# Shared low-rank factors laid out twice and rounded in three steps for four, and two unread matmuls behind the first factor mix

## Chip, cores, metric

One core of one Trainium2 chip. The metric is the device time of the whole kernel in microseconds (us), as a median over runs. PE is the matmul engine, PEld its weight loads, DVE, ACT and POOL the vector, scalar and GpSimd engines, and SP the engine whose queue issues nearly all DMA transfers.

## Reference

```
h = grouped_conv1d(x, weight) + (cond @ c_weight.T)[:, :, None] + fside[None, :, None]   # 64 rows n, 64 channels, 1024 long
A_eff = einsum('bn,nri->bri', gate, lora_A);  B_eff = einsum('bn,nor->bor', gate, lora_B)  # 8 b, rank 32
out = x + h @ kernel + bias + B_eff(A_eff h) + B_shared(A_shared h)                      # 1024 x 1024 kernel
```

The shared factors don't depend on the row, so the kernel adds B_shared · A_shared to the dense weights once (this is what `merge` does).

## The kernel before

The 64 rows are worked in 8 blocks `b` of 8 rows; each has two halves `h` of two groups `t`. Products in float32 are made from a high part (rounded to the matmul's fp32r format) and a low part (the rest): ACT rounds to the high part, DVE or POOL subtracts to get the low part, and PE makes three products, high·high, high·low and low·high. Nothing is scheduled by a program: each engine has its own queue, written out by hand, with waits on semaphores, and every engine works its queue in order.

A first stage, some 60 us long, prepares the weights while the first block is worked. Names that matter here:

- `load_la(q)`, `load_first(half)`, `load_w(ma)` on SP: loads of the per-adapter A factors (four quarters `la`), of the first block's input (`x_tr`) and of the dense weights (`w_raw`). The order on SP is small inputs, `la` 0, first half of the input, shared factors `sh_in`, `la` 1 to 3, weights 0 and 1, second half of the input, bias, weights 2 and 3, B factors.
- `mix_a(q)` (L879) on PE: quarter `q` of the gated sum of A factors into `main` (in PSUM); `a_turn(q)` on DVE turns it into `a_eff`. Quarter 0 goes to `main[1][:, 0:512]`, quarter 1 to `main[1][:, 512:1024]`.
- `x_first_high` on ACT rounds the first input into `x_hi` (two instructions of 128x528, `t` 0 and 1); `x_lo` is made for `t` 0 by DVE and for `t` 1 by POOL. `convolve` (L819) is then 12 matmuls for one tile of the convolution.
- `as_st` and `bs_st` are the two operands of `merge`. `as_st` holds rows A high, A low, A high (32 partitions each), `bs_st` B high, B high, B low, so that one matmul over 96 partitions sums the three products. `sh_in` has A in its partitions 0 to 31 and B in 32 to 63. ACT makes the four high parts in four instructions of 32 partitions (`shared_high`, L445), then POOL makes A low (`as_lo`, L339) and B low (`bs_lo`, L343).
- `merge(m)` (L867) needs all of these; DVE's `w_add(m)` adds its result to `w_raw`, ACT's `w_high(k)` and POOL's `w_low(k)` split it, and `chunk(k)` on PE uses it: 12 matmuls of 512 columns.

On PE the order at the start is: two unread matmuls on `ident`, the conditioning product, the tap transposes, `mix_a(0)`, two `convolve`, `mix_a(1)`, `mix_a(2)`, `merge(0)`, `merge(1)`, `mix_a(3)`, `merge(2)`, `merge(3)`, `chunk(0)`, and so on.

Of the kernel before, what the change touches and what calls it, by code (L numbers as in the profile page):

```python
# [8 lines left out]
ACT = mybir.ActivationFunctionType  # L9
AX = mybir.AxisListType  # L10

P = 128
# [4 lines left out]
NL, R = 16, 32  # L17
# [8 lines left out]
STACK = 3 * R  # L26
# [25 lines left out]
def adaln_ffn(nc, x, x_rows, x_first, small, conv_w, kern, bias, lora_a, lora_b, shared, out):  # L52
# [9 lines left out]
    with ctx:  # L62
# [3 lines left out]
        def ps(name, shape):  # L66
            return ctx.enter_context(nc.psum_tensor(name, shape, F32))

        def sem(name):
            return ctx.enter_context(nc.semaphore(name))  # L70

        def early(*specs):

            with ExitStack() as own:
                return [own.enter_context(nc.sbuf_tensor(*s)) for s in specs]
# [5 lines left out]
        z_all, as_st, bs_st = early(("z_all", [C, WIN, CG, J], F32), ("as_st", [P, KC, P], F32R), ("bs_st", [P, D], F32R))  # L81
        y_hi1, y_lo1 = sb("y_hi1", [P, 2, KC, P], F32R), sb("y_lo1", [P, 2, KC, P], F32R)
        sh_in, bias_nat, bias_hi, bias_lo = early(("sh_in", [P, D], F32), ("bias_nat", [16, 64], F32),
                                                 ("bias_hi", [16, 64], F32R), ("bias_lo", [16, 64], F32R))
        _, t01_raw = early(("res_front3", [P, 2, D], F32), ("t01_raw", [P, G, J, CG], F32))
        _, be_raw = early(("res_front", [P, 2, D], F32), ("be_raw", [P, RQ, 512], F32))
        _, be_lo = early(("res_front2", [P, 2, D], F32), ("be_lo", [P, RQ, 512], F32R))
        res = sb("res", [P, G, D])
        la, = early(("la", [P, RQ, L], F32))
# [19 lines left out]
        ident, gmix = early(("ident", [P, P], F32), ("gmix", [P, NB, R8], F32))  # L109
# [3 lines left out]
        main = [ps(f"main{i}", [P, D]) for i in range(2)]  # L113
# [5 lines left out]
        cw_in, small_in, shared_in = sem("cw_in"), sem("small_in"), sem("shared_in")  # L119
# [7 lines left out]
        diag_done, gmix_done, bs_hi, bs_lo = sem("diag_done"), sem("gmix_done"), sem("bs_hi"), sem("bs_lo")  # L127
        as_hi, as_lo = sem("as_hi"), sem("as_lo")
# [60 lines left out]
        def w_bank(m):  # L189
            return (spare, rank)[m % 2][:, :]  # L190
# [4 lines left out]
        def a_out(q):  # L195
            return main[1 - q // 2][:, (q % 2) * 512:(q % 2 + 1) * 512].rearrange("p (b k m) -> p b k m", b=2, m=32)
# [3 lines left out]
        def load_first(eng, half):  # L200
            m0, m1 = ((0, XSPLIT), (XSPLIT, MB))[half]
            eng.dma_start(x_tr[:, m0:m1, :, :].rearrange("p m n g -> p (m n g)"),
                          x_first[0, :, m0 * SB * G:m1 * SB * G]).then_inc(x_first_in[half], 16)
# [8 lines left out]
        def _(sp):  # L212
            sp.dma_start(sm[:, :], small).then_inc(small_in, 16)
            load_la(sp, 0)
            load_first(sp, 0)
            sp.dma_start(sh_in[0:2 * R, :], shared).then_inc(shared_in, 16)
            for q in range(1, RQ):
                load_la(sp, q)
            load_w(sp, 0)
# [28 lines left out]

            sp.wait_ge(as_lo, 1)
            sp.wait_ge(bs_lo, 1)  # L250
            sp.wait_ge(as_hi, 2)
            sp.wait_ge(bs_hi, 2)
            load_res(0, 0)
            sp.wait_ge(bias_put, 32)
# [12 lines left out]
            for i, (part, split) in enumerate(((be_hi, be_hid), (be_lo, be_lod))):  # L267
                sp.wait_ge(split, RQ)
                for oh in range(2):
                    for bq in range(2):  # L270
                        row = oh * 64 + bq * R
# [170 lines left out]
        def _(act):  # L442
            act.dma_start(w_nat[:, :], conv_w.rearrange("o c k -> o (c k)")).then_inc(cw_in, 16)

            def shared_high(q):  # L445

                row, at = ((0, R), (2 * R, 0))[q]
                nc.scalar.activation(as_st[row:row + R, :, :].rearrange("p k m -> p (k m)"), sh_in[0:R, :], ACT.Copy).then_inc(as_hi, 1)
                nc.scalar.activation(bs_st[at:at + R, :], sh_in[R:2 * R, :], ACT.Copy).then_inc(bs_hi, 1)

            for w in range(2):
                act.wait_ge(t_tr, w + 1)
                nc.scalar.activation(t_hi[:, :, w * J:(w + 1) * J, :].rearrange("p g s c -> p s g c"),
# [11 lines left out]
                                 main[0][:, 512:1024].rearrange("p (s g c) -> p s g c", s=J, g=G), ACT.Copy).then_inc(t01_copied, 1)  # L465
            x_first_high(0)
            act.wait_ge(shared_in, 16)
            shared_high(0)
            shared_high(1)

            def y_high_first(u, i, order):
                t, mh = order[i]
# [325 lines left out]
        def _(pe):  # L798
            mm = nc.tensor.matmul
# [19 lines left out]
            def convolve(b, h, i, order=ORDER, first=False):  # L819
                u = b * 2 + h  # L820
                t, mh = order[i]
                if first:

                    pe.wait_ge(x0_hi, 2 * mh + (t + 1))
                else:
                    pe.wait_ge(xlo_done, t + 1)
                if not (first and i < 2):
                    pe.wait_ge(conv_free, u * CT + (i - 1))
                n = 0
                for lhs, rhs in ((t_hi, x_hi), (t_lo, x_hi), (t_hi, x_lo)):  # L830
                    if first and rhs is x_lo:
                        pe.wait_ge((x0_lo, x0_pool)[t], mh + 1)
                    if first and lhs is t_lo:
                        pe.wait_ge(tlo_done, 2)
                    for w in range(2):
                        at = J - J * w
                        for e in range(2):
                            i0 = mh * 32 + (e + w) // 2
                            last = mm(conv[i % 2][:, e * 256:(e + 1) * 256],  # L839
                                      lhs[:, 2 * h + t, at:at + J, :].rearrange("p s c -> p (s c)"),  # L840
                                      rhs[:, t, (e + w) % 2, i0:i0 + 32, :].rearrange("p m n -> p (m n)"),
                                      start=n == 0, stop=n == 11)
                            n += 1
                last.then_inc(conv_ready, 1)
# [21 lines left out]

            def merge(m):  # L867
                if m < 2:
                    pe.wait_ge(as_hi, 2)
                    pe.wait_ge(bs_hi, 2)  # L870
                    pe.wait_ge(as_lo, 1)
                    pe.wait_ge(bs_lo, 1)
                    pe.wait_ge(ctx_done, 1)
                else:
                    pe.wait_ge(w_sum, m - 1)
                mm(w_bank(m), as_st[0:STACK, m // 2, :], bs_st[0:STACK, (m % 2) * 512:(m % 2 + 1) * 512],  # L876
                   start=True, stop=True).then_inc(w_mm, 1)

            def mix_a(q):  # L879
                pe.wait_ge(la_in[q], 16)  # L880
                if q < 2:
                    pe.wait_ge(gmix_done, 1)
                else:
                    pe.wait_ge(t01_sum, 1)
                for bh in range(2):
                    for i in range(2):
                        for jh in range(4):
                            last = mm(a_out(q)[jh * 32:(jh + 1) * 32, bh, 4 * i:4 * i + 4].rearrange("p k m -> p (k m)"),  # L888
                                      gmix[:, bh * 4:bh * 4 + 4, :].rearrange("p b r -> p (b r)"),
                                      la[:, q, :].rearrange("p (i m e h l) -> p i e l m h", i=2, m=32, e=2, h=4)[:, i, :, :, :, jh],  # L890
                                      start=True, stop=True)
                last.then_inc(a_mm, 1)
# [44 lines left out]


            mix_a(0)
            pe.wait_ge(thi_done, 2)  # L940
            convolve(0, 0, 0, FIRST, first=True)
            convolve(0, 0, 1, FIRST, first=True)
            mix_a(1)
            mix_a(2)
            merge(0)
            merge(1)
            mix_a(3)
            merge(2)
            merge(3)

# [123 lines left out]
def _laid_out(inputs, name):  # L1074

    if name == 'x_rows':

        return inputs['x'].reshape(NB, SB * G, CH, CL, L).transpose(0, 2, 1, 3, 4).reshape(NB, P, CL, L)
    if name == 'x_first':

        padded = np.pad(inputs['x'][:2 * SB], ((0, 0), (0, 0), (HALO, HALO))).reshape(2, SB, G, CH, CL, MB, J)
        return padded.transpose(0, 3, 4, 6, 5, 1, 2).reshape(2, P, MB * SB * G)
    if name == 'small':
        return np.concatenate([np.repeat(inputs['L0_ffn_gate'].T, R8, axis=0), np.tile(inputs['fside_S_0'].reshape(G, CG).T, (J, 1)),
                               inputs['cond_128'].T, inputs['L0_cond_c_weight'].T], axis=1)
    if name == 'shared':
        rows = inputs['L0_ffn_lora_A_shared'].reshape(R, 2, 32, 2, 4, 2).transpose(0, 1, 3, 5, 4, 2).reshape(R, L)
        return np.concatenate([rows, inputs['L0_ffn_lora_B_shared'].T], axis=0)
    if name == 'L0_ffn_kernel':

        return inputs[name].reshape(2, 32, 2, 4, 2, D).transpose(0, 2, 3, 1, 4, 5).reshape(4, P, 2 * D)
    return inputs[name]
# [17 lines left out]
```

## Time and profile before

| | us |
|---|---|
| median of 3 runs | 496.76 (496.27 to 497.31) |
| the profiled execution | 497.13 |
| its span, first to last instruction | 495.3 |
| PE busy in it | 486.8 |
| POOL / DVE / ACT busy | 270.6 / 319.3 / 166.9 |

The profile tells of the execution that took 497.13 us; its times count from the start of the span. "Idle before" is time in which an engine had nothing to do before an instruction, with the instruction that ended the wait. PEclk is the clock that PE was granted, as a share of 2.4 GHz. A matmul of plain float32 operands appears as two records, so the two matmuls at L804 are x4.

### The profile page before, as it was taken

The numbers are of one execution on the slowest core, as the hardware profiler recorded it, in microseconds if no ns is written. First come the engines' busy times: TensorE is split into PE (matmuls) and PEld (weight loads), VectorE is DVE, ScalarE is ACT, GpSimd is POOL, SyncE is SP. The second block draws the span as 40 slices with busy tenths as digits, with TensorE's granted clock in tenths as the row PEclk, the third lists the DMA queues.
The fourth block names the chain that finished last, engine by engine and source line by source line (L and its number), as shares of the span: only waits on it lengthen the run. The fifth ranks groups of instructions, "written<-read, shape, count | busy, mean of one in ns | idle before, by whom it ended". The sixth has DMA issues, their size and how long they took to land.

```text
span 495.3 us, 6738 instructions
## 1 busy us (share of the span) xinstructions
PE 486.8 (98%) x2417; PEld 403.1 (81%) x2417; DVE 319.3 (64%) x368; ACT 166.9 (34%) x205; POOL 270.6 (55%) x153
## 2 busy tenths in 40 slices
PE   6999999999999999999999999999999999999997
PEld 4785988888888888888888888888888888888886
DVE  4757575969667594948937595765939398473402
ACT  4575334333343152323324233431524224331100
POOL 0889865964837275661939247471846519392200
PEclk9899999999999999999999999999999999999999
DMA  8951858543624063431724245240734313241302
GB/s 252 422 233 60 255 122 226 221 134 108 218 53 125 40 232 107 106 95 29 248 72 119 71 152 183 50 129 26 249 90 113 88 36 84 63 123 66 96 32 85
DMA packets 16733, 64.56 MB, mean 130 GB/s; under 512 B 1520, under 2 KB 1968, under 8 KB 15824
## 3 DMA queue, kind: packets, MB, share of 16 engines
q1 hardware_dynamic: 16640, 64.35, 42.2%
q8 instruction: 8, 0.13, 0.1%
q10 hardware_dynamic: 80, 0.04, 0.0%
q14 instruction: 5, 0.04, 0.0%
HBM read 45.10 MB, written 18.87 MB: 129 GB/s over the span
## 4 chain that ended last, share of the span: by engine, by line
PE 97%; DMA 2%; DVE 0%; ACT 0%; SPq 0%; issue 0%
PE main L921 70%; PE rank L934 6%; PE main L926 3%; PE conv L839 3%; PE conv L863 3%; PE conv L864 3%; PE conv L865 3%; DMA x_tr<-in_x_first 2%; PE spare L865 1%; PE spare L864 1%; PE spare L863 1%; PE main L909 1%; PE main L888 1%; PE conv L901 1%; PE spare L876 0%; PE rank L876 0%
## 5 line engine op out<-in xcount | busy, mean ns | idle before, releaser
L921 PE MATMUL main<-w_hi,y_hi 128*128 128x512 f32 x504 | 155.6, 391 | 0.3 <-DVE a_eff L682 0.3
L921 PE MATMUL main<-w_lo,y_hi 128*128 128x512 f32 x504 | 155.1, 390 | 0.0
L921 PE MATMUL main<-w_hi,y_lo 128*128 128x512 f32 x504 | 154.7, 389 | 0.0
L376 POOL TENSOR_TENSOR y_lo<-y_stage,y_hi 128x512 fp32r<-128x512 f32 x56 | 93.2, 1686 | 34.3 <-ACT y_hi L479 34.3
L921 PEld LDWEIGHTS main<-w_lo,y_hi 128*128 128x128 f32 x504 | 94.5, 188 | 20.9 <-POOL w_lo L381 0.8
L921 PEld LDWEIGHTS main<-w_hi,y_lo 128*128 128x128 f32 x504 | 94.6, 188 | 19.9
L921 PEld LDWEIGHTS main<-w_hi,y_hi 128*128 128x128 f32 x504 | 93.4, 188 | 19.6 <-issue 0.7
L356 POOL TENSOR_TENSOR xd_lo<-xd,xd_hi 128x512 fp32r<-128x512 f32 x28 | 40.3, 1441 | 100.4 <-ACT xd_hi L491 100.3
L358 POOL TENSOR_TENSOR x_lo<-x_tr,x_hi 128x1024 fp32r<-128x1024 f32 x28 | 82.3, 2939 | 15.6 <-ACT x_hi L493 15.6
L493 ACT ACTIVATE x_hi<-x_tr 128x1024 fp32r<-128x1024 f32 x28 | 57.6, 2056 | 27.7 <-DVE x_tr L648 27.7
L479 ACT ACTIVATE y_hi<-y_stage 128x512 fp32r<-128x512 f32 x56 | 35.5, 634 | 91.9 <-DVE y_stage L666 91.9
L666 DVE STREAM_TRANSPOSE y_stage<-y_add 128x512 f32<-128x512 f32 x56 | 62.9, 1162 | 0.0
L738 DVE TENSOR_TENSOR ax_sum<-rank,ax_sum 32x256 f32<-32x256 f32 x16 | 6.6, 412 | 76.1 <-ACT ax_sum L504 76.1
L746 DVE TENSOR_TENSOR res<-main,res 128x1024 f32<-128x1024 f32 x31 | 37.5, 1210 | 22.9 <-PE main L926 22.9
L491 ACT ACTIVATE xd_hi<-xd 128x512 fp32r<-128x512 f32 x28 | 17.7, 633 | 90.9 <-DVE xd L644 90.9
L648 DVE TENSOR_TENSOR x_tr<-x_tr 128x512 f32<-128x512 f32 x28 | 44.7, 1597 | 1.0
L644 DVE TENSOR_TENSOR xd<-x_tr 128x512 f32<-128x512 f32 x28 | 40.0, 1428 | 1.2 <-POOL xd_lo L356 1.2
L657 DVE TENSOR_TENSOR y_add<-conv,ctx_all 128x512 f32<-128x512 f32 x28 | 19.2, 686 | 24.2 <-PE conv L865 24.2
L934 PE MATMUL rank<-y_hi,a_cur 128*64 128x256 f32 x128 | 29.9, 277 | 0.0
L934 PE MATMUL rank<-y_lo,a_cur 128*64 128x256 f32 x128 | 29.9, 277 | 0.0
L606 DVE STREAM_TRANSPOSE x_tr<-x_in 128x512 f32<-128x512 f32 (+2 forms) x48 | 29.4, 680 | 0.2
L504 ACT ACTIVATE ax_sum<-rank 32x256 f32<-32x256 f32 x16 | 6.0, 375 | 64.8 <-PE rank L934 64.8
(102 smaller groups left out, 503.3 us busy)
## 6 DMA issues: line engine op xcount, KB each, us to landing
res<-in_x SPq DMA_DIRECT2D x32, 512.0 KB
out<-res SPq DMA_DIRECT2D x31, 512.0 KB
x_in<-in_x_rows SPq DMA_DIRECT2D x6, 2048.0 KB, 12.5
w_raw<-in_L_ffn_kernel SPq DMA_DIRECT2D x4, 1024.0 KB, 16.8
b_cur<-b_scratch SPq DMA_DIRECT2D x21, 128.0 KB, 3.1
x_tr<-in_x_first SPq DMA_DIRECT2D x1, 2064.0 KB, 8.8
la<-in_L_ffn_lora_A SPq DMA_DIRECT2D x4, 512.0 KB, 10.1
lb<-in_L_ffn_lora_B SPq DMA_DIRECT2D x1, 2048.0 KB, 24.8
```

What stands on the lines that cost most here:

```text
L356: nc.gpsimd.tensor_tensor(xd_lo[:, t], xd[:, :, :], xd_hi[:, t].bitcast(F32), ALU.subtract).then_inc(xlo_done, 1)
L358: nc.gpsimd.tensor_tensor(x_lo[:, t, :, 0:NP], x_raw(2 * h + t, 0, NP), x_hi[:, t, :, 0:NP].bitcast(F32), ALU.subtract).then_inc(xlo_done, 1)
L376: nc.gpsimd.tensor_tensor(y_parity(y_lo, h, t, e), y_staged(e), y_parity(y_hi, h, t, e).bitcast(F32), ALU.subtract).then_inc(ylo_done, 1)
L479: nc.scalar.activation(y_parity(y_hi, h, t, e), y_staged(e), ACT.Copy).then_inc(yhi_done, 1)
L493: nc.scalar.activation(x_hi[:, t, :, 0:NP], x_raw(2 * h + t, 0, NP), ACT.Copy).then_inc(xhi_done, 1)
L606: nc.vector.transpose(x_tr[:, m0:m1, :, :].rearrange("p m n g -> p m (n g)"), blocks).then_inc(xt_done, 1)
L644: nc.vector.tensor_tensor(xd[:, :, :], x_block(0, 1, g), x_block(1, 0, g), ALU.subtract).then_inc(xd_done, 1)
L648: nc.vector.tensor_tensor(x_block(0, 0, g), x_block(0, 0, g), x_block(1, 0, g), ALU.subtract).then_inc(xd_done, 1)
L666: nc.vector.transpose(y_stage[:, e, :].rearrange("p (a l n c) -> p a n l c", a=2, l=2, n=SB), y_add[:, e, :].rearrange("p (a m n) -> p a n ...
L746: nc.vector.tensor_tensor(res[:, g, :], main[g % 2][:, :], res[:, g, :], ALU.add).then_inc(main_free, 1)
L921: mm(main[t][:, n * 512:(n + 1) * 512], lhs, rhs[:, k, n * 512:(n + 1) * 512], start=k == 0 and first, stop=False)
L934: last = mm(rank[0:2 * R, 0:2 * P], lhs, y[h][:, :, k, :], start=k == 0 and y is y_hi, stop=k == KC - 1 and y is y_lo)
```

## The change

The array of the shared factors is laid out twice in DRAM (128 rows for 64) and `sh_in` is loaded whole. So partitions 64 to 95 hold A again, and ACT rounds partitions 0 to 95 into `as_st` in one instruction (the middle 32, which get B's rounding there, are overwritten by POOL's A low later), then rounds B twice as before. `as_hi` is then counted once. On PE two unread matmuls on `ident` follow `mix_a(0)`; they write `main[1][:, 512:768]`, which `mix_a(1)` overwrites.

```diff
-            sp.dma_start(sh_in[0:2 * R, :], shared).then_inc(shared_in, 16)
+            sp.dma_start(sh_in[:, :], shared).then_inc(shared_in, 16)
...
-            sp.wait_ge(as_hi, 2)
+            sp.wait_ge(as_hi, 1)
...
-            def shared_high(q):
-
-                row, at = ((0, R), (2 * R, 0))[q]
-                nc.scalar.activation(as_st[row:row + R, :, :].rearrange("p k m -> p (k m)"), sh_in[0:R, :], ACT.Copy).then_inc(as_hi, 1)
-                nc.scalar.activation(bs_st[at:at + R, :], sh_in[R:2 * R, :], ACT.Copy).then_inc(bs_hi, 1)
...
-            shared_high(0)
-            shared_high(1)
+            nc.scalar.activation(as_st[0:STACK, :, :].rearrange("p k m -> p (k m)"), sh_in[0:STACK, :], ACT.Copy).then_inc(as_hi, 1)
+            for at in (R, 0):
+                nc.scalar.activation(bs_st[at:at + R, :], sh_in[R:2 * R, :], ACT.Copy).then_inc(bs_hi, 1)
...
-                    pe.wait_ge(as_hi, 2)
+                    pe.wait_ge(as_hi, 1)
...
             mix_a(0)
+            for _ in range(2):
+                mm(main[1][:, 512:768], ident[:, :], ident[:, :].unsqueeze(1).broadcast_to([P, 2, P]), start=True, stop=True)
             pe.wait_ge(thi_done, 2)
...
-        return np.concatenate([rows, inputs['L0_ffn_lora_B_shared'].T], axis=0)
+        return np.tile(np.concatenate([rows, inputs['L0_ffn_lora_B_shared'].T], axis=0), (2, 1))
```

On PE the place is the start of the program, from `mix_a(0)` (`main<-la,gmix`) to the end of the first convolution tile. Before:

```order
L888 MATMUL main<-la,gmix 32x128 x16
L839 MATMUL conv<-x_hi,t_hi 128x256 x4
L839 MATMUL conv<-x_hi,t_lo 128x256 x4
L839 MATMUL conv<-x_lo,t_hi 128x256 x4
L839 MATMUL conv<-x_hi,t_hi 128x256 x4
```

With the change:

```order
L884 MATMUL main<-la,gmix 32x128 x16
L937 MATMUL main<-ident 128x256 x2
L835 MATMUL conv<-x_hi,t_hi 128x256 x4
L835 MATMUL conv<-x_hi,t_lo 128x256 x4
L835 MATMUL conv<-x_lo,t_hi 128x256 x4
L835 MATMUL conv<-x_hi,t_hi 128x256 x4
```

Two matmuls are put between the mix and the convolution; nothing else on PE moves. On ACT the place is the rounding of the first input (`x_hi`), the shared factors behind it, and the first turned tile (`y_hi`). Before:

```order
L461 ACTIVATE x_hi<-x_tr 128x2x264 x2
L448 ACTIVATE as_st<-sh_in 32x1024
L449 ACTIVATE bs_st<-sh_in 32x1024
L448 ACTIVATE as_st<-sh_in 32x1024
L449 ACTIVATE bs_st<-sh_in 32x1024
L474 ACTIVATE y_hi<-y_stage 128x512 x2
```

With the change:

```order
L455 ACTIVATE x_hi<-x_tr 128x2x264 x2
L463 ACTIVATE as_st<-sh_in 96x1024
L465 ACTIVATE bs_st<-sh_in 32x1024 x2
L470 ACTIVATE y_hi<-y_stage 128x512 x2
```

The second rounding of A is gone, and `y_hi` stands one instruction earlier. On SP the load of `sh_in` keeps its place, between the first input's first half and `la` 1, and becomes 128x1024.

## Rows read from the trace of the kernel before

**Rows 1.** The page: busy time, share of the span and instructions of each engine

```profile
PE 486.8 (98%) x2417; PEld 403.1 (81%) x2417; DVE 319.3 (64%) x368; ACT 166.9 (34%) x205; POOL 270.6 (55%) x153
```

**Rows 2.** The chain that ended last, to 60 us: start us, us, what

```profile
1.67 8.57 DMA x_tr<-in_x_first
...
10.26 1.11 ACT x_hi L461
...
11.51 4.60 PE conv L839 x24
16.11 3.71 PE main L888 x58
...
23.33 2.08 PE main L921 x8
...
50.33 2.84 PE conv L839 x24
```

**Rows 3.** The timeline of PE: start us, us, engine, line, tiles

```profile
1.54 2.08 PE L804 MATMUL main<-ident 128*128 128x256 f32 x4 [1.54 <-POOL ident L326]
...
19.75 0.50 PE L876 MATMUL spare<-bs_st,as_st 96*128 96x512 f32 x1
...
24.34 1.08 PE L921 MATMUL main<-w_hi,y_lo 128*128 128x512 f32 x4
25.43 1.20 PE L921 MATMUL main<-w_lo,y_hi 128*128 128x512 f32 x4
```

**Rows 4.** Stretches: us, busy by engine, PEclk, DMA share, GB/s

```profile
0.00:4.80 4.80, 3.26 (x12) 2.74 (x12) 2.38 (x8) 1.28 (x1) 0.70 (x6) 1.00 0.58 129
0.00:7.60 7.60, 6.02 (x52) 4.84 (x56) 4.18 (x11) 2.38 (x3) 0.70 (x6) 1.00 0.72 222
0.00:13.40 13.40, 8.71 (x71) 7.02 (x72) 6.87 (x14) 6.09 (x8) 1.59 (x7) 0.95 0.86 266
8.00:10.50 2.50, 0.39 (x8) 0.00 (x0) 0.69 (x1) 0.71 (x2) 0.00 (x0) 1.00 1.02 217
12.00:15.40 3.40, 3.40 (x18) 3.40 (x18) 2.40 (x4) 3.35 (x4) 2.81 (x2) 0.50 1.04 423
```

**Rows 5.** The timeline of SP's queue, where loads are issued

```profile
1.22 0.41 SPq L206 DMA_DIRECT2D la<-in_L_ffn_lora_A  x1
...
2.14 0.59 SPq L216 DMA_DIRECT2D sh_in<-in_shared  x1
2.78 2.25 SPq L206 DMA_DIRECT2D la<-in_L_ffn_lora_A  x3
5.07 1.08 SPq L209 DMA_DIRECT2D w_raw<-in_L_ffn_kernel  x2
```

**Rows 6.** DMA issues in 1.25 to 1.6 us, the first factor load: count, KB, us to landing

```profile
la<-in_L_ffn_lora_A SPq DMA_DIRECT2D x1, 512.0 KB, 5.2
```

**Rows 7.** DMA issues in 2 to 2.7 us, the shared factors: count, KB, us to landing

```profile
sh_in<-in_shared SPq DMA_DIRECT2D x1, 256.0 KB, 9.5
```

**Rows 8.** DMA issues in 4.5 to 4.6 us, the fourth factor load: count, KB, us to landing

```profile
la<-in_L_ffn_lora_A SPq DMA_DIRECT2D x1, 512.0 KB, 10.9
```

**Rows 9.** DMA issues in 5.2 to 5.3 us, the first weight load: count, KB, us to landing

```profile
w_raw<-in_L_ffn_kernel SPq DMA_DIRECT2D x1, 1024.0 KB, 12.7
```

**Rows 10.** The timeline of ACT

```profile
12.31 1.04 ACT L448 ACTIVATE as_st<-sh_in 32x1024 fp32r<-32x1024 f32 x1
```

**Rows 11.** The timeline of POOL

```profile
12.51 1.58 POOL L331 TENSOR_TENSOR x_lo<-x_tr,x_hi 128x528 fp32r<-128x528 f32 x1 [11.03 <-ACT x_hi L461]
...
16.64 2.43 POOL L343 TENSOR_TENSOR bs_st<-sh_in,bs_st 32x1024 fp32r<-32x1024 f32 x1
...
22.97 2.41 POOL L381 TENSOR_TENSOR w_lo<-w_raw,w_hi 128x1024 fp32r<-128x1024 f32 x1 [1.25 <-ACT w_hi L497]
...
29.43 2.40 POOL L381 TENSOR_TENSOR w_lo<-w_raw,w_hi 128x1024 fp32r<-128x1024 f32 x1 [1.49 <-ACT w_hi L497]
```

**Rows 12.** The timeline of DVE

```profile
20.55 0.65 DVE L678 TENSOR_TENSOR w_raw<-spare,w_raw 128x512 f32<-128x512 f32 x1
```

## The prediction

> **What bounds the kernel now.** I read the page's busy times first: PE works 486.8 of 495.3 us [rows 1]. So PE is the bound, and only what delays or lengthens PE's own work counts. Next the chain that ended last, to find where PE is not simply working: from 23.33 us on it is PE piece after piece to the end, and before that it runs from the load of the first input (issued 1.67, landed 10.24), through ACT's rounding (10.26, 1.11 us), two convolution tiles (11.51, 4.60 us for 24 matmuls) and the factor mixes (16.11, 3.71 us) into `merge(0)` and `chunk(0)` [rows 2]. Everything behind is a fixed length of PE work, so a microsecond won before 23.33 is a microsecond of the total if the helpers keep up.
>
> Three things are to be seen in that opening.
>
> First, the same 24 convolution matmuls take 2.84 us at 50.33 and 4.60 us here [rows 2]. The stretch 12.0 to 15.4 us has PEclk 0.50, that is 1.2 GHz for 2.4 [rows 4]. Before it fell PE had done 0.39 us of work in the stretch 8.0 to 10.5 [rows 4] and then stood until 11.51.
>
> Second, the load. In 8.0 to 10.5 us the DMA engines are busy (share 1.02) but move only 217 GB/s, against 423 GB/s in 12.0 to 15.4 [rows 4]. What is in the queue then? Count bytes: the small inputs, `la` 0 and the first half of the input are about 0.07, 0.04, 0.52 and 1.08 MB (from the shapes), 1.71 MB. By 7.6 us 222 x 7.6 = 1.69 MB had been moved [rows 4]. So the slow stretch begins as the 64-partition load of `sh_in` comes up. How late does a load land behind the moment when its bytes are through? `la` 0: 0.63 MB are moved at about 4.85 us (129 GB/s to 4.8), it lands at 1.22 + 5.2 = 6.4, 1.6 us later [rows 4 to 6]. `la` 3: 3.55 MB at 13.4 us (266 GB/s to 13.4), it lands at about 4.28 + 10.9 = 15.2, 1.8 us later [rows 4, 5, 8]. The first input: 1.71 MB at 7.7 us, it lands at 10.24, 2.55 us later [rows 2, 4]. So the load on which PE waits is some 0.8 us later than its neighbours would be, just where the narrow load comes behind it.
>
> Third, what comes next if PE gets through the convolution sooner. `merge(0)` starts on PE at 19.75 [rows 3], at the end of the mixes. It needs B low from POOL, which ends at 16.64 + 2.43 = 19.07 [rows 11]. So PE alone can gain only 0.63 us (with 0.05 us from a POOL end to a PE start, as at `chunk(0)`: 22.97 + 2.41 = 25.38 to 25.43 [rows 3, 11]) before POOL is the wait. POOL's work goes back to the input: `x_lo` at 12.51 [rows 11] starts when ACT has rounded both halves.
>
> **The change part by part.**
>
> The two unread matmuls. The same two at the program's start take 2.08 us [rows 3]; at twice the clock they would take half, so I bound them by 1.04 and 2.08 us. They start at about 8.4, where PE falls idle, and end by 10.5 at the latest; the convolution can't start before 11.51, or 10.7 if the input lands 0.8 sooner. Cost nothing, covered by that wait. What they bring: PE's idle stretch is no longer 3.1 us but 1.0 to 2.1. If the clock then stays, the 24 matmuls take 2.84 us. They don't quite flow: the last 4 need POOL's `x_lo` (12.51 + 1.58 = 14.09), so they end at about 14.6; then the mixes, 3.71 us [rows 2], to 18.3. `merge(0)` then waits for POOL until 19.12. Gain 0.63 us. Behind that `chunk(0)` had a short wait: its second four start at 24.34, four take 0.92 us at 2.4 GHz, so its third four could start at 25.26 and start at 25.43 [rows 3], held by `w_lo(0)`. The first `w_add`, at 20.55 [rows 12], stood behind `a_turn(2)`, which now comes early; it follows `merge(0)` alone, at about 19.67. So `w_lo` comes 0.88 earlier and the matmuls 0.63: the 0.17 wait goes. Together 0.8 us.
>
> The wide load. Bytes go from 0.26 to 0.52 MB. Lower bound of its cost: it moves at 423 GB/s, the rate of 128-partition loads [rows 4], and takes 1.2 us, the same as 0.26 MB at 217 GB/s; what stands behind it is not delayed. Upper bound: it moves at 217 GB/s too and takes 1.2 us more. I take the lower one, since 12.0 to 15.4, the row of other 128-partition loads, is nearest. Then the slow stretch goes, and the first input lands like its neighbours, 1.6 to 1.8 us behind its bytes: 9.3 to 9.5, for 10.24. I take 0.8 us. All of ACT's and POOL's chain (`x_hi`, `x_lo`, A low, B low) moves with it, so PE and POOL both gain 0.8.
>
> The Trainium skill (SBUF — State Buffer, "Door 1: The DMA port swizzle") says that partitions 0 to 63 reach only 8 of 16 ports, so such a load has half the rate. By this rule the wide load takes as long as the narrow one. The trace agrees with its 217 against 423 GB/s, but the slow stretch lasts 2.5 us, twice what 0.26 MB at half rate explains, so the rule is not the whole of it; by the rule's own 1.2 us alone the input might gain less, perhaps 0.4.
>
> Does `sh_in` itself come in time? It landed at 2.14 + 9.5 = 11.64 [rows 5, 7] and ACT took it at 12.31 [rows 10], now 11.5. Its bytes are through at 7.7 + 1.25 = 8.95, plus 1.8 is 10.8: yes. The first weights landed at 5.07 + 12.7 = 17.8 [rows 5, 9]; they are wanted at 19.67 - 0.8 = 18.87. Even with 0.26 MB more at 423 GB/s (0.62 us, were there nothing to win back) they are there at 18.4. Hidden.
>
> Three roundings for four. One of 32x1024 takes 1.04 us [rows 10], and partitions go in parallel, so I price 96 partitions the same; at worst they take three times that, 3.1 us. At 1.04 ACT is free 1.05 us sooner, but POOL's A low waits for the first rounding and B low for the second, which keep their places; `y_hi` behind them feeds POOL's `y_lo`, which stands behind B low anyway. Gain nothing. At 3.1 us `merge(0)` would come 2 us later; the row speaks against that, since ACT's `x_hi`, on all 128 partitions, takes 1.11 us [rows 2] and not four times a rounding on 32.
>
> Later: POOL's `w_lo(2)` starts at 29.43 out of a wait of 1.49 us for ACT [rows 11], which waits for `merge(5)` behind `chunk(0)`. So POOL's long busy run moves with PE, and nothing eats the gain.
>
> Sum: 0.8 (clock) + 0.8 (load) = 1.6 us. The profiled execution took 497.13, so 495.5 for such a one. It stands 0.37 above the median of the runs shown; the medians compared, 496.76 - 1.6 = 495.2.
>
> **The rivals.**
>
> *Load no earlier, clock held.* The 0.8 us come from the queue's own jitter and not from `sh_in`; the slow stretch being longer than it explains speaks for it. Gain 0.8: 496.0.
>
> *Load earlier, clock falls at 12.0 all the same.* The convolution starts at 10.7, does 1.3 us at full clock, the rest in twice the time, to 15.1; mixes to 19.0, `merge(0)` 0.8 to 0.9 earlier. 495.9. Against it: PE is then busy from 8.4 to 9.4 at least and again from 10.7.
>
> *Nothing happens.* Clock falls, load as before: 496.8.
>
> *Slower.* The wide load takes 1.2 us more at 217 GB/s and shares the engines with the tail of the first input, which lands at 11.4. PE then idles over 2 us even behind the unread matmuls, the clock falls, and all moves 1.2 later: 498.0. It decides from a landing 1.0 us late. For it: loads do overlap, since the input lands long after its bytes should be through; against it: 423 GB/s for wide loads.
>
> **How the numbers follow.** Both 0.50; load no earlier 0.24; clock falls 0.08; nothing 0.10; slower 0.08. About 0.2% (1.0 us) is what a measurement of this kernel can tell from no change. Of the first case I count 0.44 as over 1.0 us (a load 0.2 us earlier is enough, less for the scatter of runs), of the second 0.07, of the third 0.03: faster 0.54. Slower 0.07 from the last; the rest, 0.39, is no change. Time: the likeliest case, 495.2. Range: below, 0.96 us for the load (a lag of 1.6) and half the scatter of the runs shown (0.4) give 494.6; above, it takes in "nothing", 496.9; "slower" is left out.
>
> **What would show it.** PEclk 1.00 throughout 12.0 to 15.4 and 24 convolution matmuls in about 3.2 us. The first input landing at 9.3 to 9.5, no stretch at 217 GB/s. `merge(0)` at 18.3, out of a short wait for POOL, and `chunk(0)` at 21.9. One 96x1024 rounding of 1.05 us. I am wrong if the input lands at 10.2 or later, if the clock falls, or if the weights come after 19 us and DVE waits for them.

## The result

| | us | against before |
|---|---|---|
| before, 18 runs | 496.81 median (495.50 to 498.86) | |
| changed, 18 runs | 495.50 median (495.38 to 496.01) | 0.9974 (0.9966 to 0.9983) |
| changed, the profiled execution | 495.48, span 493.6 | 497.13, span 495.3 |

The changed kernel is 1.3 us (0.26%) faster. What the single median does not tell: the runs of before spread over 3.4 us, those of the changed kernel over 0.6. Before reaches 495.5 too in its best execution, and is 1 to 3 us longer in most.

The timeline of PE in the changed kernel, to hold against [rows 2, 3]:

```profile
7.17 1.99 PE L884 MATMUL main<-la,gmix 128*32 128x128 f32 x32
9.09 1.13 PE L937 MATMUL main<-ident 128*128 128x256 f32 x4
10.41 0.71 PE L835 MATMUL conv<-x_hi,t_hi 128*128 128x256 f32 x4 [0.18 <-ACT x_hi L455]
...
13.05 0.74 PE L835 MATMUL conv<-x_lo,t_hi 128*128 128x256 f32 x4
13.72 3.75 PE L884 MATMUL main<-la,gmix 128*32 128x128 f32 x64
18.21 0.47 PE L872 MATMUL spare<-bs_st,as_st 96*128 96x512 f32 x1 [0.73 <-POOL bs_st L343]
...
21.80 1.16 PE L917 MATMUL main<-w_hi,y_hi 128*128 128x512 f32 x4 [0.28 <-DVE a_eff L678]
...
23.70 1.18 PE L917 MATMUL main<-w_lo,y_hi 128*128 128x512 f32 x4
```

The convolution starts at 10.41 for 11.51. Its 24 matmuls need 3.3 us (10.41 to 13.7) for 4.60. The mixes end at 17.5, and `merge(0)` starts at 18.21 out of a wait of 0.73 us for POOL, where it stood at 19.75 and waited for nothing. `chunk(0)` starts at 21.80 for 23.33, 1.53 us earlier; its third four matmuls start at 23.70 for 25.43, 1.73 us earlier, and the span is 1.7 us shorter.

Stretches of the changed kernel, in the columns of [rows 4]:

```profile
8.00:10.50 2.50, 2.32 (x29) 1.29 (x22) 1.49 (x3) 1.87 (x3) 0.00 (x0) 1.00 1.02 416
12.00:15.40 3.40, 3.40 (x46) 2.79 (x49) 3.05 (x5) 3.02 (x4) 3.32 (x2) 1.00 1.04 436
```

The slow stretch of the queue is gone: 416 GB/s for 217 in 8.0 to 10.5 us. PEclk is 1.00 for 0.50 in 12.0 to 15.4, and here the durations of the matmuls bear it out (what PEclk shows before its first recorded change is taken up at the end). PE is busy 2.32 us in 8.0 to 10.5 us for 0.39, which is the end of the first mix, the unread matmuls and the start of the convolution.

The two loads, issued at 1.67 and 2.14 us, with the us from issue to landing as the last number:

```profile
x_tr<-in_x_first SPq DMA_DIRECT2D x1, 1056.0 KB, 7.4
```

```profile
sh_in<-in_shared SPq DMA_DIRECT2D x1, 512.0 KB, 8.2
```

The first input lands at 1.67 + 7.4 = 9.07 (10.24 before), and twice the bytes of shared factors land at 2.14 + 8.2 = 10.3 (11.6 before).

POOL's timeline and the first roundings on ACT:

```profile
11.39 1.61 POOL L331 TENSOR_TENSOR x_lo<-x_tr,x_hi 128x528 fp32r<-128x528 f32 x1 [9.91 <-ACT x_hi L455]
13.08 2.40 POOL L339 TENSOR_TENSOR as_st<-sh_in,as_st 32x1024 fp32r<-32x1024 f32 x1
15.56 2.39 POOL L343 TENSOR_TENSOR bs_st<-sh_in,bs_st 32x1024 fp32r<-32x1024 f32 x1
...
21.24 2.39 POOL L381 TENSOR_TENSOR w_lo<-w_raw,w_hi 128x1024 fp32r<-128x1024 f32 x1 [0.64 <-ACT w_hi L493]
```

```profile
8.63 0.60 ACT L458 ACTIVATE t_raw<-main 128x512 f32<-128x512 f32 x1 [0.76 <-DVE t_lo L595]
9.13 2.18 ACT L455 ACTIVATE x_hi<-x_tr 128x528 fp32r<-128x528 f32 x2
11.19 1.07 ACT L463 ACTIVATE as_st<-sh_in 96x1024 fp32r<-96x1024 f32 x1
```

POOL goes with hardly a gap from 11.39 to the end of B low at 17.95, and PE takes `merge(0)` 0.26 us later. ACT starts `x_hi` at 9.13, just behind its copy of the taps (8.63 + 0.60 = 9.23, the marks overlap by some 0.1 us): the load is no longer alone in setting this start.

### The profile page after: what moved, and what is told of

Its sections match the earlier page's. It is cut to its first block, busy times and chain, and to the rows that moved or that the text cites. A ratio compares the mean times of both kernels' runs of the same rounds, so it can differ in the third digit from the quotient of the medians.

```text
span 493.6 us, 6745 instructions
## 1 busy us (share of the span) xinstructions
PE 487.3 (99%) x2421; PEld 403.1 (82%) x2421; DVE 319.1 (65%) x368; ACT 166.0 (34%) x204; POOL 270.5 (55%) x153
## 4 chain that ended last, share of the span: by engine, by line
PE 97%; POOL 1%; ACT 1%; issue 1%; DVE 0%; POOLq 0%
PE main L917 70%; PE rank L930 6%; PE main L922 3%; PE conv L859 3%; PE conv L860 3%; PE conv L861 3%; PE conv L835 2%; PE spare L861 1%; PE spare L860 1%; PE spare L859 1%; PE main L905 1%; PE conv L897 1%; POOL bs_st L343 0%; PE spare L872 0%; ACT x_hi L455 0%
```

## The experiments

Each was timed beside the kernel before on its chip; medians of before were 497.11 (runs 1 to 4), 497.28 (5 to 8) and 497.05 (9 to 12), so ratios are what compares between groups. For every execution the mean granted clock of its span is on record too: the profiles in which the clock fell have 0.993 to 0.997, the others 0.998 or more, so this figure tells how often it fell. It does not tell of a full clock that comes late at the start, as in run 3.

| run | median us | to before (95%) | landed, us (profile) | 8.0 to 10.5, GB/s |
|---|---|---|---|---|
| before (its profile above) | | | 10.24 | 217 |
| 10 before again (one run) | 497.94 | | 10.9 | 220 |
| 1 unread matmuls only | 496.53 | 0.9990 (0.9976 to 1.0003) | 8.9 | 261 |
| 11 the same (one run) | 497.01 | | 10.7 | 205 |
| 2 wide load only | 495.52 | 0.9968 (0.9954 to 0.9982) | 9.3 | 420 |
| 3 wide load, three roundings | 495.74 | 0.9971 (0.9958 to 0.9984) | 9.4 | 420 |
| 12 unread, wide, four roundings | 495.67 | 0.9974 (0.9962 to 0.9986) | 8.6 | 418 |
| 8 changed kernel again | 495.85 | 0.9973 (0.9963 to 0.9983) | 9.0 | 416 |
| 5 narrow load later | 499.43 | 1.0046 (1.0030 to 1.0062) | 9.4 | 422 |
| 6 changed, 96 rows loaded | 496.45 | 0.9991 (0.9978 to 1.0003) | 9.7 | 246 |
| 9 unread, 64 rows to partitions 32 to 95 | 495.67 | 0.9975 (0.9962 to 0.9987) | 9.5 | 417 |
| 4 changed, B low on DVE | 496.32 | 0.9982 (0.9970 to 0.9995) | 9.7 | 418 |
| 7 changed, input low part on DVE | 494.97 | 0.9962 (0.9946 to 0.9977) | 9.1 | 420 |

"Landed" is the landing of the first input, 1.67 us and the time to landing.

### The parts of the change

**1. Unread matmuls only** (edit on before):

```diff
             mix_a(0)
+            for _ in range(2):
+                mm(main[1][:, 512:768], ident[:, :], ident[:, :].unsqueeze(1).broadcast_to([P, 2, P]), start=True, stop=True)
```

> The kernel before with only the two unread matmuls behind the first factor mix. If clock and load are two separate gains, this has the first alone: the first input lands at about 10.2, PEclk stays 1.00 through 12.0 to 15.4, the 24 convolution matmuls take about 3.2 us (2.84 and a short wait for POOL's low part), merge(0) starts at about 19.1 out of a wait for POOL, and the time is 0.6 to 0.8 us below before. Rival, the clock stays only because the input lands earlier and shortens the wait: here the clock falls at about 12.0 and the time is that of before. Rival, the clock was not worth anything in most executions of before: PEclk is 1.00, but the median is within 0.3 us of before.

The ratio, 0.9990, is not told from 1. The profiled execution took 495.63 us, as fast as the changed kernel, and shows why one execution misleads. Its stretch 8.0 to 10.5:

```profile
8.00:10.50 2.50, 2.32 (x29) 1.48 (x20) 1.49 (x3) 1.87 (x3) 0.00 (x0) 1.00 1.03 261
```

The slow stretch is there, and yet the input landed at 1.67 + 7.2 = 8.9. So the input can land early with the narrow load behind it too. Of the 13 executions of this kernel (run 11 with them) one shows a fall of the clock, against 44 of the 86 executions of before that were timed beside the runs. Those 44 have a median of 497.54 us and the other 42 one of 496.72.

**11. The same kernel again.**

> The kernel before with the unread matmuls only, one more look. PEclk stays 1.00 through 10 to 18 us whatever the landing of the first input; if that is after 9.2, the whole of ACT's and POOL's chain and the time follow it one for one.

This execution took 497.01 us. ACT and PE:

```profile
10.70 2.16 ACT L461 ACTIVATE x_hi<-x_tr 128x528 fp32r<-128x528 f32 x2 [1.61 <-DMA x_tr<-in_x_first]
```

```profile
8.97 1.57 PE L941 MATMUL main<-ident 128*128 128x256 f32 x4
11.95 0.71 PE L839 MATMUL conv<-x_hi,t_hi 128*128 128x256 f32 x4 [1.40 <-ACT x_hi L461]
...
19.76 0.47 PE L876 MATMUL spare<-bs_st,as_st 96*128 96x512 f32 x1 [0.75 <-POOL bs_st L343]
```

The input landed at 10.7, 1.8 us later than in run 1, and ACT waited 1.61 us for it; the convolution starts 1.54 later (11.95 for 10.41), `merge(0)` 1.56 later (19.76 for 18.20), the whole 1.38 later. The clock did not fall in either.

**10. The kernel before again.**

> The kernel before, one more look. The slow stretch at 8.0 to 10.5 us is there in every execution; what differs between fast and long ones is when the first input lands (8.9 to 10.3) and whether the clock falls behind PE's wait. [...]

```profile
12.13 0.72 PE L839 MATMUL conv<-x_hi,t_hi 128*128 128x256 f32 x4 [2.98 <-ACT x_hi L461]
...
13.27 1.17 PE L839 MATMUL conv<-x_lo,t_hi 128*128 128x256 f32 x4
...
20.52 0.50 PE L876 MATMUL spare<-bs_st,as_st 96*128 96x512 f32 x1
```

It took 497.94 us. The input landed at 10.9, PE waited 2.98 us, and the clock fell, though only at 13.0. Held against run 11, where the input came 0.2 us earlier and the clock held: 0.9 us of difference, so the fallen clock costs about 0.7 (an estimate from one execution of each).

**2. Wide load only** (edit on before; the array is laid out twice, as in the change):

```diff
-            sp.dma_start(sh_in[0:2 * R, :], shared).then_inc(shared_in, 16)
+            sp.dma_start(sh_in[:, :], shared).then_inc(shared_in, 16)
```

> The kernel before with only the shared factors laid out twice and loaded to 128 partitions; four roundings, no unread matmuls. If the narrow load held up the first input: it lands at about 9.1, 8.0 to 10.5 us moves over 400 GB/s, PE starts the convolution at about 10.4. The wait of PE is then 2 us for 3.1; if that alone keeps the clock, the time is that of the changed kernel (1.3 us below before), if the clock falls the gain is 0.5 to 0.9 us. Rival, the whole gain is the clock's: within 0.2 us of before.

This has the whole gain, 0.9968, with 10 of 11 runs from 495.34 to 496.09 and one at 496.65, the only one with a fall of the clock (mean 0.996). PE in its profile:

```profile
10.57 0.71 PE L839 MATMUL conv<-x_hi,t_hi 128*128 128x256 f32 x4 [1.34 <-ACT x_hi L461]
...
18.39 0.48 PE L876 MATMUL spare<-bs_st,as_st 96*128 96x512 f32 x1 [0.81 <-POOL bs_st L343]
```

PE waits 1.34 us for ACT, and the convolution runs at the full clock without the unread matmuls.

**3. Wide load and three roundings** (edit on the changed kernel):

```diff
             mix_a(0)
-            for _ in range(2):
-                mm(main[1][:, 512:768], ident[:, :], ident[:, :].unsqueeze(1).broadcast_to([P, 2, P]), start=True, stop=True)
```

> The changed kernel without the two unread matmuls: wide load and three roundings. If the third rounding is hidden, as forecast, it has the time of the wide load with four roundings within 0.2 us, and merge(0) starts at the same time; ACT is free 1.05 us sooner. Rival, that ACT instruction is on the path: 0.3 us or more below the one with four roundings.

0.9971, the same as with four. Its profiled execution was a long one, 496.76 us (the other ten runs are 495.49 to 496.13):

```profile
10.69 1.19 PE L835 MATMUL conv<-x_hi,t_hi 128*128 128x256 f32 x4 [1.38 <-ACT x_hi L455]
11.68 1.05 PE L835 MATMUL conv<-x_hi,t_lo 128*128 128x256 f32 x4
...
19.35 0.49 PE L872 MATMUL spare<-bs_st,as_st 96*128 96x512 f32 x1
```

```profile
12.00:15.40 3.40, 3.40 (x19) 3.40 (x19) 1.99 (x3) 2.67 (x3) 3.32 (x2) 1.00 1.04 435
```

PE waited 1.38 us, nearly as long as in run 2, and both inputs landed within 0.1 us of each other, yet the executions differ by 1.1 us: the first five groups of four matmuls take 1.00 to 1.19 us for 0.63 to 0.74. This is not a clock that fell behind the wait. PEclk shows 1.00 in the whole stretch, and the trace's first record of the full clock is at 15.06 us, just where the sixth group speeds up to 0.63; in run 2 that record is at 9.36. So in this execution PE was still at the lower of its two levels, 1.2 GHz, until 15.06. A wait of 1.34 us in run 2 and of 1.39 in run 5 did no harm.

Do the unread matmuls prevent such an execution? That is not shown. Over 496.2 us lie 2 of the 22 runs of the wide load without them, one with a fall and one with the late full clock, and none of the 42 with them (the changed kernel's 18 and 12, and 12 of run 12); but 2 of the 12 of run 9, which has them and no slow stretch either, lie there too, and in its profile the full clock came only at 11.17.

**12. Four roundings.** The changed kernel with the four roundings of before.

> The changed kernel with four roundings for three: unread matmuls and wide load. If the fourth rounding is hidden, the median is that of the changed kernel, 495.5 to 495.9, merge(0) starts 0.7 us after PE falls idle, out of a wait for POOL, and only y_hi starts about 1 us later. Rival, y_hi on ACT delays POOL's y_lo or w_hi(0): 0.3 us or more above.

0.9974, the changed kernel's own ratio. `merge(0)` starts at 18.22 for 18.21, `y_hi` at 15.53 for 14.46. The third rounding is hidden.

**8. The changed kernel again.**

> The changed kernel itself, on the same chip as the three others, as their measure. The time is 495.5 within 0.2 us, spread under 1 us; the first input lands at 9.1 to 9.7.

The median is 495.85 where 495.3 to 495.7 was expected, at the same ratio as before (0.9973); all runs lie in 495.40 to 496.00.

### What makes the queue slow

**5. The narrow load behind the fourth factor load** (edit on before):

```diff
-            sp.dma_start(sh_in[0:2 * R, :], shared).then_inc(shared_in, 16)
             for q in range(1, RQ):
                 load_la(sp, q)
+            sp.dma_start(sh_in[0:2 * R, :], shared).then_inc(shared_in, 16)
```

> The kernel before with the narrow load of the shared factors issued behind the fourth factor load, no other change. If the narrow load makes the slow stretch of the queue, 8.0 to 10.5 us runs above 400 GB/s, the first input lands at 9.1 to 9.4, and a stretch of 1.2 to 2.5 us at 220 to 260 GB/s comes later, from about 11.5 us. The shared factors then land about 2.5 us later, at some 14, so POOL's A low starts only after 15 and merge(0) at about 20.2: the time is 0 to 0.7 us above before. Rival, the slow stretch belongs to the place in the queue (the second factor load, or a start-up effect): it stays at 8.0 to 10.5 us.

```profile
8.00:10.50 2.50, 1.22 (x24) 0.58 (x16) 1.30 (x2) 1.75 (x3) 0.00 (x0) 1.00 1.03 422
...
11.50:15.00 3.50, 3.50 (x39) 2.83 (x41) 3.16 (x5) 0.03 (x1) 1.58 (x1) 1.00 1.06 254
```

The slow stretch moved with the load: 422 GB/s where it stood, 254 GB/s in 11.5 to 15.0, and PE's wait of 1.39 us for the input brought no fall. The first input landed at 9.4. The time was missed: the shared factors landed at 15.5 and not 14, ACT waited 4.05 us for them, B low ended at 21.6 and PE waited 4.1 us. In that wait the clock fell as well: PEclk is 0.50 from 19.7 to 26.5, and the two matmuls of `merge(0)` take 0.76 and 0.63 us for 0.50 and 0.40 in before. All ten executions show a fall. The time is 2.2 us above before where 0 to 0.7 was expected.

**6. 96 rows loaded for 128** (edit on the changed kernel; the array has 96 rows too):

```diff
-            sp.dma_start(sh_in[:, :], shared).then_inc(shared_in, 16)
+            sp.dma_start(sh_in[0:STACK, :], shared).then_inc(shared_in, 16)
```

> The changed kernel with 96 rows of the shared factors loaded for 128, which is all that is rounded. If what counts is how the bytes lie over SBUF's ports, partitions 64 to 95 relieve nothing: partitions 0 to 63 still hold 0.26 MB, and a slow stretch of 1 to 2.5 us below 330 GB/s stands in 8.0 to 10.5 us; the median is 0.3 to 1.0 us above the changed kernel, and the spread is that of before. Rival, what counts is that more than 64 partitions are written: no slow stretch, time of the changed kernel within 0.2 us.

The slow stretch is back at 246 GB/s, and with it a part of the loss: 496.45, 0.6 us above the changed kernel on the same chip. No execution shows a fall of the clock, so these 0.6 us are not a fall's.

**9. 64 rows, but to partitions 32 to 95.** On the kernel before with the unread matmuls:

```diff
-            sp.dma_start(sh_in[0:2 * R, :], shared).then_inc(shared_in, 16)
+            sp.dma_start(sh_in[R:3 * R, :], shared).then_inc(shared_in, 16)
...
-                row, at = ((0, R), (2 * R, 0))[q]
+                row, at = ((2 * R, R), (0, 0))[q]
```

A and B are swapped in the array, and A low is made from partitions 64 to 95.

> Unread matmuls as in the changed kernel, four roundings, and the narrow load of 64 rows (0.26 MB) written to partitions 32 to 95 for 0 to 63, with A and B swapped; all else as before. If the slow stretch comes from partitions 0 to 63 lying on one half of SBUF's ports, this load has 32 partitions on each half: no stretch below 350 GB/s in 8.0 to 10.5 us, or a short one, the first input lands at about 9.0, and the time is that of the wide load, 495.5 to 495.9. Rival, a load of fewer than 128 partitions is slow wherever it lies: the slow stretch of 2 us or more stays, and the median is that of the unread matmuls alone, 0.6 us or more above.

```profile
8.00:10.50 2.50, 2.50 (x31) 1.73 (x24) 1.38 (x2) 1.73 (x3) 0.00 (x0) 1.00 1.02 417
```

The same 64 rows and 0.26 MB as in run 1, one start partition changed, and the queue runs at 417 GB/s; the ratio is that of the wide load. So it is where the rows lie, and neither their number (run 6) nor their bytes. This is the port rule of the Trainium skill (SBUF — State Buffer, "Door 1: The DMA port swizzle"): partitions 0 to 63 are one half of the ports, 32 to 95 reach both. The runs agree with it, and they show that the second copy of the shared factors was not needed for the speed.

**How the narrow load reaches the one before it.** The traces keep every packet of the queue, and these divide the delay of the first input in two. From the end of its last packet to its landing it takes 0.32 to 0.35 us in each of the nine profiles that have no slow stretch right behind it, and 0.58 to 0.87 us in each of the five that have one (0.78 in before, 0.34 in the changed kernel). That is some 0.4 us in every execution. The end of the last packet itself scatters: 8.3 to 9.3 us in the nine, 8.1 to 10.1 in the five.

The length of the slow stretch is seen a little better too. In 2.5 us at 217 GB/s, 0.54 MB pass, twice the narrow load, and the packets of 4 KB in it take about 300 ns for 159 in the changed kernel. So about as many bytes of the factor load behind are slowed with it. Why is not shown.

### What PE waits for now

**4. B low on DVE** (edit on the changed kernel; POOL's instruction goes):

```diff
             y_tile(0, 0, 1, FIRST, first=True)
+            dve.wait_ge(bs_hi, 1)
+            nc.vector.tensor_tensor(bs_st[2 * R:STACK, :], sh_in[R:2 * R, :], bs_st[R:2 * R, :].bitcast(F32),
+                                    ALU.subtract).then_inc(bs_lo, 1)
             a_turn(1)
```

> The changed kernel with B low made by DVE, behind the second turned tile, in place of POOL. If POOL's chain (low part of the input, A low, B low) is what PE waits for before merge(0), the wait of 0.73 us goes: DVE starts it at about 16.1 and needs about 1.1 us, merge(0) starts when the mixes end, at about 17.4, and the time is 0.5 to 0.8 us below the changed kernel, 494.8 to 495.0. Rival, w_add(0) on DVE or w_low(0) on POOL takes the wait's place at chunk(0): less than 0.3 us.

```profile
16.58 1.91 DVE L698 TENSOR_TENSOR bs_st<-sh_in,bs_st 32x1024 fp32r<-32x1024 f32 x1
18.51 1.32 DVE L674 STREAM_TRANSPOSE a_eff<-main 128x512 f32<-128x512 f32 x2
19.86 0.69 DVE L670 TENSOR_TENSOR w_raw<-spare,w_raw 128x512 f32<-128x512 f32 x1
```

```profile
16.09 3.53 POOL L360 TENSOR_TENSOR y_lo<-y_stage,y_hi 128x512 fp32r<-128x512 f32 x2
```

No gain: 0.9982 of before where the changed kernel has 0.9974, with intervals that overlap, so no loss is told either; the rival won. B low takes 1.91 us on DVE, not the 1.1 expected; beside it POOL's two `y_lo` take 3.53 us for 2.58 in the changed kernel. PE still waits 0.62 us for B low. Behind it two turns stand before `w_add(0)`, which starts 1.4 us after the end of B low (19.86 to 18.49) for 0.8 in the changed kernel (18.78 to 17.95). So `w_hi(0)` comes late, and at `chunk(0)` PE waits 0.50 us for it and 0.20 for `w_lo(0)`. In this execution the input also landed 0.6 us later than in the changed kernel's.

**7. The input's low part on DVE** (edit on the changed kernel; POOL's `x_first_low(0)` goes, and `a_turn(2)` moves behind the first two `w_add`):

```diff
             x_first_low(0)
+            dve.wait_ge(x0_hi, 2)
+            nc.vector.tensor_tensor(x_part(x_lo[:, 1], 0), x_raw(1, *x_half(0)),
+                                    x_part(x_hi[:, 1], 0).bitcast(F32), ALU.subtract).then_inc(x0_pool, 1)
             a_turn(0)
...
             a_turn(1)
-            a_turn(2)
             w_add(0)
             w_add(1)
+            a_turn(2)
             a_turn(3)
```

> The changed kernel with POOL's low part of the first input's first half made by DVE, right behind DVE's own, and DVE's order changed to a_turn(1), w_add(0), w_add(1), a_turn(2), a_turn(3). POOL's chain before merge(0) is then two instructions for three and starts at about 12.3: B low ends at 17.2, merge(0) starts at about 17.4 at the end of the mixes, with no wait for POOL, and the time is 0.6 to 0.8 us below the changed kernel. Rival, as with B low on DVE: DVE and POOL slow each other where both read two operands from SBUF, or DVE's queue holds w_add(0) back: gain under 0.3 us.

```profile
17.55 0.47 PE L871 MATMUL spare<-bs_st,as_st 96*128 96x512 f32 x1
...
21.12 1.17 PE L916 MATMUL main<-w_hi,y_hi 128*128 128x512 f32 x4 [0.28 <-DVE a_eff L674]
```

```profile
12.41 2.40 POOL L335 TENSOR_TENSOR as_st<-sh_in,as_st 32x1024 fp32r<-32x1024 f32 x1 [10.92 <-ACT as_st L459]
14.89 2.41 POOL L339 TENSOR_TENSOR bs_st<-sh_in,bs_st 32x1024 fp32r<-32x1024 f32 x1
```

```profile
11.41 1.11 DVE L694 TENSOR_TENSOR x_lo<-x_tr,x_hi 128x528 fp32r<-128x528 f32 x1
...
18.13 0.69 DVE L670 TENSOR_TENSOR w_raw<-spare,w_raw 128x512 f32<-128x512 f32 x1 [0.80 <-PE spare L871]
```

DVE makes the low part in 1.11 us while POOL stands idle until 12.41, where in run 4 the two worked side by side. The wait of 0.73 us is gone: `merge(0)` starts at 17.55, when the mixes end, and `chunk(0)` at 21.12 for 21.80. The median is 494.97, 0.9 us below the changed kernel on the same chip (0.6 to 0.8 expected) and the fastest of all: 0.9962 of before. Its slowest run (495.34) is below the changed kernel's fastest there (495.40).

## Why the prediction was right, and where it was off

**What bounds it.** Right. A microsecond before `chunk(0)` was a microsecond of the total: there PE is 1.53 us earlier and the profiled execution 1.65 us shorter. The rest is the wait for `w_lo(0)` inside `chunk(0)`, put at 0.17 us: its third four matmuls now follow without it, 1.73 us earlier.

**The path of one execution.** Nearly to the point, for an execution like the one profiled: `merge(0)` at 18.3 (18.21), `chunk(0)` at 21.9 (21.80), 24 convolution matmuls in 3.2 us (3.3), 495.5 us (495.48). That `merge(0)` fits so well is in part luck: the input landed at 9.07, some 0.3 us before the 9.3 to 9.5 forecast, and from the end of B low on POOL to `merge(0)` went 0.26 us (17.95 to 18.21) where 0.05 was counted.

**The wide load.** The lower cost, no delay, was right, and run 5 shows the cause, the slow stretch going where the narrow load goes. The first input landed between 8.6 and 9.7 us in the nine profiles without a slow stretch around its landing, and at 8.9, 9.7, 10.2, 10.7 and 10.9 in the five with it. So 0.8 us is a fair mean (9.2 against 10.1) of something that varies by 2 us: about half of it is the steady 0.4 us between last packet and landing, the other half the scatter of the last packet, which five profiles are too few to price. The slow stretch of 2.5 us for 0.26 MB was noted as longer than the port rule explains; 64 and 96 rows gave about the same stretch. Its length is still not explained.

**The unread matmuls: the mis-sized term.** The sum gave them 0.8 us by themselves. Without the wide load they are worth 0.1% or 0.5 us in the median, not told from nothing (run 1, interval from 0.24% faster to 0.03% slower), and on top of it nothing (0.9968 and 0.9971 without, 0.9973 and 0.9974 with). The price of a fallen clock was right where it falls: 0.7 us from runs 10 and 11, and 0.8 between the medians of before with and without a fall (late loads may have their part in that one). What failed is the step that took one execution's two losses as two terms to be added up for the median. The clock fell in 44 of 86 executions of before, not in all, so it can't be counted in full for the median. And the fall hung on PE's long wait for the late load, which either part shortens: it is left in 1 of 13 executions with the unread matmuls alone and in 1 of 22 with the wide load and no unread matmuls (PE's wait was 1.3 to 1.4 us in their profiles). So either part ends it nearly always: the second has no fall left to win, and the wide load by itself has the whole gain.

**Their cost.** Right: bounded by 1.04 and 2.08 us, and 1.13 measured, hidden behind the wait for the input. They start at 9.09 and not at 8.4: the transposes ahead of them took 1.97 us for the 1.21 of the one profile that the forecast was made from.

**The median.** 1.6 us was forecast and 1.3 measured. The sum started from an execution 0.37 us above the median shown, with late load and fallen clock both, and took the whole sum off that median.

**Three roundings for four.** Right: 1.07 us for 96 partitions, and no gain (run 12).

**Slower, and nothing eats the gain.** The wide load ran at the full rate, so the slower case had no ground. POOL's `w_lo(2)` moved along (27.68 for 29.43), as forecast. The wait of PE for POOL before `merge(0)` was forecast too, and run 7 shows its worth.

## What to carry to other kernels

A narrow load can slow a load that was issued before it. Look at GB/s beside the DMA share: here a full share at half the rate (1.02, 217 GB/s) went with a load on partitions 0 to 63, and moving its start partition cured it without more bytes. Where the runs of a kernel scatter, two losses seen in one execution are not to be added up for the median; look at a second execution, or price each loss by how often it occurs. And when a wait goes, ask at once what stands 0.7 us behind it: here POOL's queue, and moving one instruction to DVE, where DVE had a gap and POOL stood idle, and one turn behind the adds gave another 0.9 us.

## What the hardware showed unexpectedly

**The clock at the start.** PEclk shows 1.00 from the start in every profile until the first fall, yet the same transposes of the taps (x16) took 1.21 us in the first profile of before and 1.97 in all others, and the unread matmuls 1.13 us in the changed kernel but 2.04 in run 9:

```profile
9.30 2.04 PE L941 MATMUL main<-ident 128*128 128x256 f32 x4
10.81 1.00 PE L839 MATMUL conv<-x_hi,t_hi 128*128 128x256 f32 x4
11.65 0.64 PE L839 MATMUL conv<-x_hi,t_lo 128*128 128x256 f32 x4
```

Half the speed fits the lower of the two clock levels. The traces keep the moments at which the grant changed, which the views show only as a mean. The first record of the full clock stands at 5.16 us in the first profile of before, 8.86 in the changed kernel, 8.6 to 9.9 in ten others, 11.17 in run 9 and 15.06 in run 3, and each agrees with the matmuls around it. What sets this moment is not shown. So until its first recorded change the row's 1.00 is not to be trusted; durations of equal matmuls are. It matters here: in the changed kernel ACT's copy of the taps, 0.7 us later for it, and the landing come together, at 9.2 and 9.1.

**The changes come late.** In run 10 PE did its first work at the lower clock, was granted the full one at 9.60, when it had stood idle for some 0.4 us, stood 2.98 us in all, worked at full speed from 12.13 on, and the clock fell at 13.0, in the middle of the work.
